# One transformer block, eight cores: all stores moved from the GpSimd DMA queue to the SyncE queue, and the K, Q and V loads the other way

## The reference

```python
xn = layernorm(x)
q, k, v = split(xn @ w_qkv)                    # 16 heads of 64
q, k = rope(rmsnorm(q)), rope(rmsnorm(k))
s = softmax(q @ k.T / 8) @ v @ w_proj + b_proj
h = silu(xn @ (w_gate / 127).T) * (xn @ (w_up / 127).T)
g = silu(h @ (w_down / 127).T)
out = x + s * g
```

## Time and profile before

| | us |
|---|---|
| median of 2 runs | 9660.8 |
| the two runs | 9530.7, 9791.0 |
| profiled execution | 9513.6 |
| its span on the slowest core (core 2) | 9512.0 |

### The profile page before, as it was taken

The page is one execution under the profiler, slowest core; times in us unless marked ns, Lnnn a source line. Parts: engine busy times, 40 slices in busy tenths (PEclk is TensorE's granted clock), DMA queues, the critical chain, the costliest instruction groups (busy, mean ns, idle before and its releaser), DMA issues.

```text
span 9512.0 us, 106026 instructions; the slowest of 8 cores (9466.3 to 9512.0 us)
## 1 busy us (share of the span) xinstructions
PE 6365.6 (67%) x37008; PEld 2187.6 (23%) x37008; DVE 3389.1 (36%) x5281; ACT 4962.1 (52%) x5281; POOL 354.6 (4%) x660
## 2 busy tenths in 40 slices
PE   0233237787788877777887778787777767777722
PEld 0011112222222222222222222232222222222210
DVE  2444444433433334433334334433434442111122
ACT  0000006656656656656666656666655557878700
POOL 1000000000000000000000000000000000000000
PEclk9755558888888888888888888888887778888866
DMA  8411222122212221122222221122122120000043
GB/s 250 142 66 65 83 95 64 49 74 69 71 60 66 67 73 58 57 66 78 63 66 67 60 84 56 56 85 73 50 60 76 44 87 11 2 24 2 2 128 102
DMA packets 468150, 655.01 MB, mean 69 GB/s; under 512 B 76468, under 2 KB 297652, under 8 KB 462516
## 3 DMA queue, kind: packets, MB, share of 16 engines
q1 hardware_dynamic: 433332, 547.53, 19.4%
q0 software_dynamic: 34304, 100.71, 2.9%
HBM read 530.59 MB, written 117.44 MB: 68 GB/s over the span
## 4 chain that ended last, share of the span: by engine, by line
PE 46%; DVE 18%; ACT 17%; issue 8%; DMA 8%; SPq 1%; DVEq 0%; ACTq 0%; POOL 0%; POOLq 0%
PE ps_b L238 13%; ACT big L839 12%; PE ps_s L238 11%; PE ps_pv L238 9%; PE ps_a L238 8%; PE ps_z L238 5%; DVE zi L889 4%; DMA big<-x_fm 2%; ACT big L669 1%; DVE big L663 1%; DMA big<-v_scr 1%; ACT big L666 1%; SPq L233 1%; DVE big L608 1%; DMA big<-wuT 1%
## 5 line engine op out<-in xcount | busy, mean ns | idle before, releaser
L839 ACT ACTIVATE big<-ps_s,cbias 128x1024 bf16<-128x1024 f32 x4096 | 4241.8, 1140 | 1771.0 <-PE ps_s L238 1758.6
L238 PE MATMUL ps_s<-big 64*128 64x512 bf16 (+1 forms) x8704 | 1841.0, 412 | 971.4 <-ACT big L839 651.9
L238 PE MATMUL ps_pv<-big 128*64 128x512 bf16 x8192 | 1783.6, 432 | 68.3 <-ACT big L839 68.3
L238 PE MATMUL ps_b<-big 128*128 128x512 bf16 x4608 | 1250.6, 426 | 0.0
L238 PEld LDWEIGHTS ps_s<-big 64*128 64x128 bf16 (+1 forms) x8704 | 505.8, 94 | 2239.7 <-issue 2185.6
L238 PE MATMUL ps_a<-big 128*128 128x128 bf16 (+1 forms) x5632 | 720.0, 291 | 307.0 <-DMA big<-ropes 282.1
L238 PE MATMUL ps_z<-big,onesb 128*1 128x512 bf16 x8192 | 840.4, 400 | 0.0
L238 PEld LDWEIGHTS ps_pv<-big 128*64 128x64 bf16 x8192 | 461.7, 109 | 1102.4 <-issue 1102.4
L238 PEld LDWEIGHTS ps_b<-big 128*128 128x128 bf16 x4608 | 453.4, 106 | 681.8 <-issue 332.1
L238 PEld LDWEIGHTS ps_a<-big 128*128 128x128 bf16 x5632 | 434.1, 109 | 567.4 <-issue 447.0
L238 PE MATMUL ps_z<-zeros 128*128 128x512 bf16 (+1 forms) x256 | 97.3, 380 | 628.4 <-DVE zib L891 575.1
(11 more groups left out here) (121 smaller groups left out, 3864.4 us busy)
## 6 DMA issues: line engine op xcount, KB each, us to landing
big<-xn_scr SPq DMA_DIRECT2D x1088, 128.0 KB, 3.1
big<-x_fm SPq DMA_DIRECT2D x192, 256.0 KB, 4.6
big<-wg_bf SPq DMA_DIRECT2D x192, 256.0 KB, 2.7
big<-wu_bf SPq DMA_DIRECT2D x192, 256.0 KB, 2.7
big<-wd_bf SPq DMA_DIRECT2D x192, 256.0 KB, 3.1
big<-ropec SPq DMA_DIRECT2D x128, 256.0 KB, 3.8
big<-ropes SPq DMA_DIRECT2D x128, 256.0 KB, 4.6
xn_scr<-big POOLq DMA_DIRECT2D x128, 128.0 KB, 2.1
```

The source lines that it names most:

```text
L238: return e.matmul(o, l, r, start=st, stop=sp, tile_position=tp)
L839: ev_exp[c] = ac(lambda e, c=c, so=so, p=p: e.activation(out=pr6(c), in_=ps_s[:, so:so + 1024], func=AF.Exp, bias=cbias[:, p:p + 1], scale ...
```

## The change

Each `dma("gp", ...)` becomes `dma("sy", ...)`: the stores of all stages and the two small copies cflip and crow. The three loads of K, Q and V become `dma("gp", ...)`. Semaphores, waits, sizes and the order of the program stay as they are. So 656 DMAs (all that POOL issued) go into SP's list at their place in the program, and 24 go from SP's to POOL's.

```diff
-            ev_bst0[sl] = dma("gp", "gbst%d" % sl, wqkv_scr[c], bst[sl][:, 0:3072],
+            ev_bst0[sl] = dma("sy", "gbst%d" % sl, wqkv_scr[c], bst[sl][:, 0:3072],
...
-            ev_bst[slot] = dma("gp", "gbst%d" % slot, dst, bt, waits=[ec])
+            ev_bst[slot] = dma("sy", "gbst%d" % slot, dst, bt, waits=[ec])
...
-                        ev_kq_free = dma("gp", "gkq", dstt[:, t0:t0 + TT],
+                        ev_kq_free = dma("sy", "gkq", dstt[:, t0:t0 + TT],
...
-                    ev_v_free = dma("gp", "gv", v_scr[p][:, t0:t0 + TT],
+                    ev_v_free = dma("sy", "gv", v_scr[p][:, t0:t0 + TT],
...
-                ef1 = dma("gp", "gcf", cflip[p:p + 1, :], kmax[0:2, p:p + 1],
+                ef1 = dma("sy", "gcf", cflip[p:p + 1, :], kmax[0:2, p:p + 1],
...
-                ef2 = dma("gp", "gcf", crow[:, 2 * p:2 * p + 2], cflip[p:p + 1, :],
+                ef2 = dma("sy", "gcf", crow[:, 2 * p:2 * p + 2], cflip[p:p + 1, :],
...
-                ev_sp = dma("gp", "gxn", xn_scr[c * 128:(c + 1) * 128, t0:t0 + TT],
+                ev_sp = dma("sy", "gxn", xn_scr[c * 128:(c + 1) * 128, t0:t0 + TT],
...
-                    ev_gst_free = dma("gp", "gg", g_scr[dd][:, f0:f0 + 512],
+                    ev_gst_free = dma("sy", "gg", g_scr[dd][:, f0:f0 + 512],
...
-            ek = dma("sy", "skv%d" % sl, kb[:, 0:NTOT], kt_scr[p], waits=wld)
-            eq = dma("sy", "skv%d" % sl, qb[:, 0:NOWN], q_scr[p])
-            evv = dma("sy", "skv%d" % sl, vb[:, 0:NTOT], v_scr[p])
+            ek = dma("gp", "skv%d" % sl, kb[:, 0:NTOT], kt_scr[p], waits=wld)
+            eq = dma("gp", "skv%d" % sl, qb[:, 0:NOWN], q_scr[p])
+            evv = dma("gp", "skv%d" % sl, vb[:, 0:NTOT], v_scr[p])
...
-                    st["ost_free"] = dma("gp", "go", o_scr[p][:, q0:q0 + QT],
+                    st["ost_free"] = dma("sy", "go", o_scr[p][:, q0:q0 + QT],
```

## The result

| | before | after |
|---|---|---|
| median of all runs, us | 9710.9 (10 runs) | 10311.4 (11 runs) |
| profiled execution, us | 9513.6 | 10272.9 |
| ratio after to before | | 1.0729, 95% interval 1.0672 to 1.0785 |

The forecast was 10145 us with a range of 9900 to 10430 and "slower". The changed kernel is 7.3% slower.

A forecast was written before the change was run, and what follows sets the result against it. It took issue order, not bandwidth, as the bound outside the first stage: SP works in order and stands at waits. 9512 plus 185 (stage 1), 161 (layernorm), 277 (attention), 8 (K, Q, V) and 1.6 gave 10145 us, range 9900 to 10430.

The forecast's parts named there:

- Stage 1: Dequantisation of weights: each next load goes out only behind a store, so casts stand further apart; +185 us (150 to 299).
- Layernorm: Layernorm stage: x_fm loads and first projection loads stand behind stores of earlier tiles; +161 us (90 to 200).
- The term of x_fm: Layernorm stage: x_fm loads behind the v store idle the chain 9.0 us at 13 tiles, 117; tiles 1 and 2 add 11.
- the first reloads: Layernorm stage: first projection tile gets its weight and reload slots late, 20 us; the next two tiles together 19.
- Attention: Attention stage: each projection tile's reload stands behind the previous tile's v store, so PE waits; +277 us (100 to 380).
- 72: Attention while the gate generator runs: 37 tiles with short gaps get late reloads, with three stragglers; +72 us.
- the 56 for pair starts: Attention, 7 pair starts: 24 weight slots stand ahead of the first reload, 8 us taken for each; +56 us.
- the sum of 149 for 21 tiles: Attention after the gate work: 21 tiles with a 2.48 us gap have reloads 7.1 us late each; +149 us.
- K, Q, V on POOL: Loads at pair ends: POOL reacts later and its slot is longer, with the rate unchanged; +1 us at each of 8, +8.
- rival 3: K, Q, V loads are slow on POOL: +360 us on top, 10505 us in all; chance 0.10.
- Rival 1: Queue choice doesn't matter since loads could pass a waiting store; only POOL's reaction changes, about 9520 us; chance 0.03.
- Rival 2: Attention absorbs most late reloads and only about 40 us at pair starts stay; 9908 us in all; chance 0.17.

The follow-up runs named there:

- e6: The changed kernel with stage 1's loads of block i+2 put ahead of the store of block i, stores still on SP; 10098 to 10248 us.
- e7: The changed kernel with the reload of a projection tile issued one tile ahead, before the current tile's K store; 9866.9 us profiled, ratio to before 1.0351.
- e4: The kernel before with only the 128 spill stores to xn_scr moved to SP; 9503.3 us profiled.
- e3: The kernel before with only the projection's stores (K, Q, V, cflip, crow) moved to SP; 9880.6 us profiled.
- e5: The kernel before with only the 64 stores to g_scr and the 64 to o_scr moved to SP; 9660.8 us in one execution.
- e1: The kernel before with only the three loads of K, Q and V moved to POOL; 9611.7 us profiled.
- e13: The kernel before with the projection one tile behind the layernorm and 19 more generator steps taken before attention; ratio to before 0.9831.

## Why the prediction was right

**The rule.** "No load can be issued before the last result that stands ahead of it in the program" held in every stage. e6 and e7 prove it from the other side: the same stores on the same queue, with the loads put ahead of them in the program, cost nothing in stage 1 (313 us against 311) and some 15 us in pairs 5 and 6. The Trainium skill (DMA: Bandwidth & Descriptors, section Issuing engines are not separate DMA queues) says that the choice of the issuing engine saves only the sequencer's time for the issue, usually little. The runs agree as far as the transfers go (from the K load to the first matmul 16.9 us from SP in before, 16.5 from POOL in after); they don't where entries wait: the choice costs 7.3% here.

**Stage 1: predicted +185, measured +161.** The casts of wgT and wuT stand 5.67 us apart (99.2 to 365.7, 47 steps) instead of the 5.94 predicted; w_qkv has 11.16 instead of 10.6, wdT 11.86 instead of 12.6. The wgT load lands in 4.4 us at the median, where I had taken 4.6. (By its own terms the low bound for wgT and wuT is +100, not +103; nothing rests on it.)

**Layernorm: predicted +161, measured +206.** The term of x_fm was right: DVE waits for it 151 us against 117 + 11 predicted. e4 and e3 show the two halves (25.6 and 126.2 us of such waits). The rest is in the reloads. PE's waits for ropes grow from 281 us (12 waits) to 373 (18). By time, core 5 of after, 472 to 800 us, 800 to 1700 and the last stretch before the first score:

```profile
PE ps_a L238 <- DMA big<-ropes: 61.6, 4, 32.5
...
PE ps_a L238 <- DMA big<-ropes: 268.9, 12, 22.9
...
PE ps_a L238 <- DMA big<-ropes: 42.2, 2, 31.3
```

The twelve in the middle are as long as those of before (22.4 us each against 23.4), so the prediction was right to take the reload as covered there. The term that was too small is that of the first reloads: 39 for three tiles, where PE waits 61.6 us at four, 32.5 of them at the first (predicted 20). The last two waits, 31.3 and 11.0 us, were not in it at all. Not all of this is on the path, since 151 + 92 is more than 206; how much is, no run shows.

**Attention: predicted +277, measured +309 inside the pairs.** That the two are near is in part luck: two terms were off, with opposite signs. The stores of K, Q and V alone (e3) give 50 + 180 = 230, not 277. While the gate work lasts that is 50 where 72 and part of the 56 for pair starts were put; in after PE waits there 81 us (40 waits). After the gate work the sum of 149 for 21 tiles met 135 us of waits (24) in e3 and 160 (27) in after. The failed step is that the stores to g_scr and o_scr had no term in the sum, as if they cost nothing: they add 76 (e5). Their store waits on SP for its DVE result, and a reload behind it is late too; I had looked at the gate weight loads behind them, but not at the reloads.

**PE's clock: not in the prediction.** Between pairs 4 and 6 the waits come to 160 us, yet the stretch is 206 us longer. PE's matmuls, the same in number, take 54 us more (1354 to 1408). In e3 it is 1402 us, so 49 of its 180 us are this and not waits: the terms of the prediction were all waits, and they met a sum that waits alone don't make. The section on the hardware below has the row.

**K, Q, V on POOL: predicted +8, measured -7 in seven pair changes.** Their sum is about 126 us before and 119 after (core 5), so the low end was right and rival 3 wrong. That the part costs nothing holds only in company: by itself it costs 108 us (e1). The prediction followed the wait of the K load and didn't ask which entry stands ahead of it on POOL's list. That the o_scr store left this list in the same change saved the term; that was luck.

**The rivals.** Rival 1 (the queue doesn't matter) fell with the first cast interval. Rival 2 (attention hides its part) put 40 us and fell with the 309. Measured on core 5 the sum is 676 against the 631 predicted: -24 in stage 1, +45 in layernorm, +32 inside the pairs and -15 at the pair changes, and some 8 us behind pair 6, which are within the scatter. The profiled execution took 10272.9 us, 759 more than before. The slowest core (core 3) took 121 us longer than core 5, and its granted clock was lower (0.783 against 0.807), which the prediction didn't consider.

## What to carry to other kernels

A DMA queue that also carries loads should hold no command that waits for a result younger than the next load needs; if loads and stores must share one, the order of the program has to put the next loads ahead of the store, and then sharing was nearly free in stage 1 and in pairs 5 and 6. Where a load waits itself for a young result, as the reload of the layernorm stretch does for its spill, this doesn't help. When a transfer is moved, look at what stands ahead of it in its new list at its moment: the same loads cost 108 us behind one store and nothing without it. And a long wait of the load queue is worth a look by itself: here it pointed to the 1.7% that e13 gains.

## What the runs showed of the hardware

A wait of PE cost more than its length here. After the 5.84 us wait at 8184 us shown above, the granted clock was 0.50, the lower of the two levels (1.2 GHz), and the eight matmuls took 3.57 us; in the kernel before they followed other matmuls at 1.00 (2.4 GHz) and took 1.90. Core 5 of after, then core 2 of before:

```profile
8184.40:8188.00 3.60, 3.60 (x10) 1.08 (x10) 0.00 (x0) 0.00 (x0) 0.00 (x0) 0.50 0.00 0
```

```profile
7869.45:7871.35 1.90, 1.90 (x12) 0.77 (x10) 0.00 (x0) 1.21 (x2) 0.00 (x0) 1.00 0.00 0
```

From the end of pair 4 to that of pair 6 it is 54 us in 8367 matmuls, a third on top of the waits, and e7, which takes the waits away, gives the clock back. In the stretch before it this isn't clear: PE is busy 4062 us in after and 4060 in e7, which hardly waits there, against 4024 in before and 4045 in e4.

The software queue, POOL's, was not slower with the large transfers of K, Q and V: its 41.94 MB took 1.1% of 16 engines' span (10271 us), 23.2 bytes per ns and engine, and the hardware queue, SP's, made 19.1. POOL did react later. The K load of a pair waits for the last matmul of the pair before, as the copy L866 does: on core 5 SP issued it 0.02 us before the start of that copy (before, 8355.63) and POOL 0.77 us after it (after, 9024.82).
